# Attention operands as two float32r stacks on half the partitions each, scores and maxima in alternating row tiles, three score banks, and outputs kept transposed

## What is computed

```python
x = x + _layernorm(_L0_attn_ref(_layernorm(x), qkv_w, qkv_b, out_w, out_b))
x = x + _layernorm(_L0_ffn_ref(_layernorm(x), W1, b1, W2, b2))
...
# _L0_attn_ref: 16 heads of 16
qkv = x @ qkv_w.T + qkv_b
scores = einsum('bhqd,bhkd->bhqk', q, k) / sqrt(16)
attn = softmax(scores, axis=-1)
out = einsum('bhqk,bhkd->bhqd', attn, v)
return out.reshape(B, S, E) @ out_w.T + out_b
```

## Time and profile before

| | us |
|---|---|
| median of 3 runs | 2549.8 (2549.22 to 2554.26) |
| the profiled execution | 2556.4 |
| its span, first to last instruction | 2554.6 |
| phase_qkv | 0 to 119 |
| phase_attention, first instruction at 119.5, first scores at 175.3 | 119 to 987 |
| phase_project_ffn | 987 to 1250 |
| the rest | 1250 to 2555 |

### The profile page before, as it was taken

One profiled execution on the slowest core, in us unless ns is written; L12 is line 12 of the kernel. 1 busy time (PEld: TensorE's weight loads), 2 busy tenths in 40 slices (PEclk: granted clock), 3 DMA queues, 4 the chain that ended last, 5 costly groups with the idle time before them and its releaser, 6 DMA issues. The chain is left out here.

```text
span 2554.6 us, 41316 instructions
## 1 busy us (share of the span) xinstructions
PE 2278.0 (89%) x14644; PEld 1462.9 (57%) x14644; DVE 1613.1 (63%) x2762; ACT 1345.3 (53%) x2589; POOL 644.6 (25%) x407
## 2 busy tenths in 40 slices
PE   7779999999999994787579999999999999588886
PEld 4412222222222222676568888888888888477775
DVE  5588788877878852677435445454545534568876
ACT  5517777777777773454254344444434444354551
POOL 3400000000000000355423325233332523234432
PEclk9859999999999997898789999999999999799998
DMA  6831211211121002111330213121220311200100
GB/s 193 241 77 54 55 40 39 73 41 39 39 73 41 6 7 88 34 50 50 120 100 26 93 38 105 52 67 52 67 93 28 115 51 59 66 17 26 33 17 25
DMA packets 129296, 159.02 MB, mean 62 GB/s; under 512 B 29896, under 2 KB 111952, under 8 KB 125008
## 3 DMA queue, kind: packets, MB, share of 16 engines
q1 hardware_dynamic: 129104, 156.47, 20.6%
HBM read 117.76 MB, written 38.27 MB: 61 GB/s over the span
## 5 line engine op out<-in xcount | busy, mean ns | idle before, releaser
L509 DVE TENSOR_REDUCE att_sb_mx<-att_ps_psM 128x1 f32<-128x1024 f32 x512 | 608.4, 1220 | 151.0 <-PE att_ps_psM L567 143.7
L667 ACT ACTIVATE att_sb_pt<-att_ps_psS 128x512 f32<-128x512 f32 x1024 | 586.2, 598 | 209.4 <-PE att_ps_psS L574 193.7
L574 PE MATMUL att_ps_psS<-att_sb_q,att_sb_k 99*128 99x512 bf16 x1024 | 392.7, 386 | 30.5 <-ACT att_sb_pt L667 12.0
L574 PEld LDWEIGHTS att_ps_psS<-att_sb_q,att_sb_k 99*128 99x128 bf16 x1024 | 96.9, 96 | 458.4 <-ACT att_sb_pt L667 406.4
L567 PE MATMUL att_ps_psM<-att_sb_k,att_sb_q 96*128 96x512 bf16 x1024 | 321.2, 396 | 28.5 <-DVE att_sb_ident_b L503 23.2
L582 PE MATMUL att_ps_psO<-att_sb_pt,att_sb_v 128*32 128x512 f32 x2048 | 273.9, 607 | 1.0 <-ACT att_sb_pt L667 1.0
L163 POOL MEMSET ffn_sb_half<- 128x4 f32 x1 | 0.1, 107 | 853.5 <-POOLq L184 853.5
L1922 ACT ACTIVATE gla_sb_sg<-gla_ps_psP 128x512 f32<-128x512 f32 x64 | 38.2, 598 | 277.1 <-PE gla_ps_psP L1683 277.1
L2256 POOL TENSOR_TENSOR gla_sb_dm<-gla_sb_dm,gla_sb_masked 128x1024 f32<-128x1024 f32 x64 | 158.5, 2498 | 90.5 <-DMA gla_sb_dm<-decay_rows 90.2
L1939 ACT ACTIVATE gla_sb_dm<-gla_sb_dm,gla_sb_neg_g 128x128 f32<-128x128 f32 x512 | 156.4, 391 | 10.1 <-POOL gla_sb_dm L2256 10.1
L567 PEld LDWEIGHTS att_ps_psM<-att_sb_k,att_sb_q 96*128 96x128 bf16 x1024 | 99.1, 100 | 107.7 <-DVE att_sb_mx L509 31.3
(11 more groups left out here) (256 smaller groups left out, 4917.0 us busy)
## 6 DMA issues: line engine op xcount, KB each, us to landing
gla_sb_dm<-decay_rows SPq DMA_DIRECT2D x32, 1024.0 KB, 5.8
gla_sb_eg<-decay_exp SPq DMA_DIRECT2D x64, 256.0 KB, 6.7
qk_parts<-qkv_sb_part SPq DMA_DIRECT2D x64, 192.0 KB, 3.1
values<-qkv_sb_va SPq DMA_DIRECT2D x32, 256.0 KB, 3.5
att_sb_v<-values SPq DMA_DIRECT2D x32, 256.0 KB, 3.7
att_sb_q<-qk_parts SPq DMA_DIRECT2D x32, 192.0 KB, 3.1
att_sb_k<-qk_parts SPq DMA_DIRECT2D x32, 192.0 KB, 3.0
qkv_sb_xin<-in_x SPq DMA_DIRECT2D x8, 512.0 KB, 5.1
```

The costliest lines, as they stand in the source:

```text
L509: nc.vector.tensor_reduce(mx[:, t // NT, t % NT:t % NT + 1], psM[:, t % 2, :], AX.X, ALU.max).then_inc(maxima_free, 1)
L574: pe.matmul(psS[:, j % 2, :], k[0:ROWS, g, j, s * P:(s + 1) * P], q[0:ROWS, g, qh, j, :], start=True, stop=True).then_inc(scores_done, 1)
L667: nc.scalar.activation(pt[:, s % 2, j, :], psS[:, j % 2, :], ACT.Exp).then_inc(exp_done, 1)
```

## The change

- phase_qkv multiplies in float32r: weights and turned inputs are split in a high and a low part, and three passes (high x high, high x low, low x high) replace one float32 matmul. q and k leave in two float32r parts in place of three bfloat16 ones, the low one made by DVE from PSUM; GpSimd's part falls away. `part` has two buffers. The scale of 1/4 moves to the exponential.
- phase_attention stacks three blocks of 16 rows (48) and two rows of maxima, 50 in all, once on partitions 0 to 49 and once on 64 to 113: heads 0 and 2 of a group below, 1 and 3 above. The k side has -1 on the rows of the maxima, set by memsets ahead of the loads.
- Each step issues scores in the order of heads 0, 2, 1, 3, and behind each of them one half (512 keys) of a maxima tile on the other row half. L582's group stands behind the third of them. psS has three banks; the maxima's rows are turned into one of these at step 5.
- Maxima run one and a half units ahead.
- GpSimd splits the maxima in two parts. Outputs are not turned: SP spreads the row of sums over partitions (four DMAs), DVE takes the reciprocal, SP stores it in DRAM and reads it back spread over 32 partitions for each head (four DMAs), and GpSimd multiplies `osb` with it. SP stores the result as it lies, features on partitions.
- phase_project_ffn reads its operand turned already; `turn_projected` and `copy_projected` go.

```diff
-Q_PART = (0, 1, 2, 0, 0, 1)
-K_PART = (0, 1, 0, 1, 2, 0)
+Q_PART = (0, 0, 1)
+K_PART = (0, 1, 0)
-ROWS = STACK + 3
+ROWS = STACK + 2
+HALF_PE = P // 2
...
+        PASSES = ((whi, xhi), (whi, xlo), (wlo, xhi))
...
                     for k in range(KD):
-                        mm = pe.matmul(psQ[:, mt, :], w[:, k, mt * P:(mt + 1) * P], xT[:, u, k, :],
-                                       start=(k == 0), stop=(k == KD - 1))
+                        for p, (wp, xp) in enumerate(PASSES):
+                            mm = pe.matmul(psQ[:, mt, :], wp[:, k, mt * P:(mt + 1) * P], xp[:, u, k, :],
+                                           start=(k == 0 and p == 0), stop=(k == KD - 1 and p == 2))
...
-        part = m.sb("part", [P, 4, 3, ST], BF16)
+        part = m.sb("part", [P, 2, 4, 2, ST], F32R)
...
-        q = m.sb("q", [P, NG, QH, HG, ST], BF16)
-        k = m.sb("k", [P, NG, HG, SEQ], BF16)
+        q = m.sb("q", [P, NG, QH, 2, ST], F32R)
+        k = m.sb("k", [P, NG, 2, SEQ], F32R)
-        psS = m.ps("psS", [P, 2, ST])
+        psS = m.ps("psS", [P, 3, ST])
-        psX = m.ps("psX", [P, NT, P])
...
+            def sums(u, w):
+                sp.wait_ge(osb_ready, u + 1)
+                for j in range(HG):
+                    sp.dma_start(den[VW * j:VW * (j + 1), w, :], osb[VW * j:VW * j + 1, w, :]).then_inc(den_in, 16)
+                sp.wait_ge(rden_ready, u + 1)
+                sp.dma_start(dens[w].rearrange("(p c) -> p c", p=P), rden[:, w, :]).then_inc(rden_out, 16)
+                sp.wait_ge(rden_out, 16 * (u + 1))
+                for j in range(HG):
+                    sp.dma_start(rb[VW * j:VW * (j + 1), w, :],
+                                 dens[w, j * ST:(j + 1) * ST].rearrange("(a c) -> a c", a=1).to_broadcast([VW, ST])
+                                 ).then_inc(rb_in, 16)
...
+            def body(b, g, last):
+                for qh in range(QH):
+                    start = isinstance(b, int) and b == 0 and g == 0 and qh == 0
+                    pb, pg, pq = (b, g, 0) if qh else ((b, g - 1, 1) if g else (b - 1, NG - 1, 1))
+                    if not start:
+                        sums(unit(pb, pg, pq), pq)
+                    nb, ng = (b, NG - 1) if g == 0 else (b + 1, g - 1)
+                    if qh == 0 and not (isinstance(nb, int) and nb >= BATCH):
+                        load_first(nb, ng, minus_set[ng] if start else None)
+                        load_second(nb, ng)
+                    if not (last and qh == 1):
+                        rows(*unit_after(b, g, qh), None if start else unit(pb, pg, pq))
...
+                    if not start:
+                        out(pb, pg, pq)
...
+            def maxima_half(b, g, qh, t, c):
+                u = unit(b, g, qh)
+                r, j, n = 1 - t % 2, t // 2 // NT, t // 2 % NT
+                rs = slice(HALF_PE * r, HALF_PE * r + STACK)
+                if c == 0:
+                    wait_past(pe, maxima_taken, TILES * u + t - 1)
+                mm = pe.matmul(psM[:, t % 2, c * ST:(c + 1) * ST], q[rs, g, qh, j, n * P:(n + 1) * P],
+                               k[rs, g, j, c * ST:(c + 1) * ST], start=True, stop=True)
+                if c == QH - 1:
+                    mm.then_inc(maxima_done, 1)
...
+            def scores(b, g, qh, s, i, turning):
+                u, pos = unit(b, g, qh), place(s, i, turning)
+                r, j = ORDER[i] % 2, ORDER[i] // 2
+                rs = slice(HALF_PE * r, HALF_PE * r + ROWS)
...
+                pe.matmul(psS[:, ring_slot(pos), :], k[rs, g, j, s * P:(s + 1) * P], q[rs, g, qh, j, :],
+                          start=True, stop=True).then_inc(ring_done, 1)
...
+                        for i in range(HG):
+                            scores(b, g, qh, s, i, not final)
+                            t = AHEAD + 2 * s + i // 2
+                            if t < TILES:
+                                if not final:
+                                    maxima_half(*nxt, t, i % 2)
+                            elif not last:
+                                maxima_half(*nxt2, t - TILES, i % 2)
+                            if i == 2:
                                 if s:
-                                    values(g, u, s - 1)
+                                    values(b, g, qh, s - 1)
...
+            def normalize(u, w):
+                pool.wait_ge(rb_in, 64 * (u + 1))
...
+                nc.gpsimd.tensor_tensor(on[:, w, :], osb[:, w, :], rb[:, w, :], ALU.mult).then_inc(on_ready, 1)
```

More of the change, by code:

```diff
@@ L265, in _ @@
             s = Steps(LN)
[L266 to L272, removed]
@@ L284, in body @@
+            stats_of_x(0, 0)
+            normalize_x(0, 0)
+            dve.wait_ge(whi_ready, 1)
+            nc.vector.tensor_tensor(wlo[:, :, :], w[:, :, :], whi[:, :, :], ALU.subtract).then_inc(wlo_ready, 1)
+            take_turned(0, 0)
+            dve.wait_ge(b_ready, 32)
+            dve.wait_ge(va_set, 4)
             def body(i, u, last):
                 if not last:
[L286 to L300, removed]
+                    stats_of_x(i + 1, 1 - u)
@@ L302, in _ @@
+                for mt in range(2):
+                    low_part(i, u, mt)
+                if not last:
+                    normalize_x(i + 1, 1 - u)
+                for mt in range(2, 4):
+                    low_part(i, u, mt)
+                if not last:
+                    take_turned(i + 1, 1 - u)
+                for pair in range(2):
+                    take_values(i, u, pair)
             over_supertiles(dve, body)
@@ L539, in _, with reciprocal @@
-            for qh in range(QH):
-                maxima(0, 0, qh, range(TILES))
-                split_maxima(0, 0, qh)
+                    if t == 0 and not (isinstance(u, int) and u < 2):
+                        dve.wait_ge(split, 2 * (u - 1))
+                    nc.vector.tensor_reduce(mx[:, qh, 8 * r + c:8 * r + c + 1], psM[:, t % 2, :], AX.X,
+                                            ALU.max).then_inc(maxima_taken, 1)
+            def reciprocal(u, w):
+                dve.wait_ge(den_in, 64 * (u + 1))
+                nc.vector.reciprocal(rden[:, w, :], den[:, w, :]).then_inc(rden_ready, 1)
@@ L660, in body, with exponentials @@
+            def exponentials(u, s, i, turning):
+                pos = place(s, i, turning)
+                act.wait_ge(ring_done, HG * (KT * u + s) + i + 1)
+                if i == 0:
+                    wait_past(act, pv_done, KT * u + s - 1)
+                nc.scalar.activation(pt[:, s % 2, ORDER[i], :], psS[:, (pos + 1) % 3, :], ACT.Exp,
+                                     scale=AD ** -0.5).then_inc(ring_taken, 1)
+            copy_rows(0, 0)
             def body(b, g, last):
                 for qh in range(QH):
-                    u = 2 * (NG * b + g) + qh
+                    u = unit(b, g, qh)
+                    start = isinstance(b, int) and b == 0 and g == 0 and qh == 0
+                    final = last and qh == 1
@@ L670, in body @@
-                        if s == 3 and not (last and qh == 1):
-                            copy_rows(u + 1)
+                        if s == TURN_AT and not final:
+                            copy_rows(u + 1, (HG * s + 1) % 3)
+                        for i in range(HG):
+                            exponentials(u, s, i, not final)
+                            if s == 0 and i == 2 and not start:
+                                copy_outputs(u - 1, 1 - qh)
             over_pairs(act, body)
-            copy_outputs(2 * NBG - 1)
+            copy_outputs(2 * NBG - 1, 1)
@@ L998, in _ @@
         def _(act):
-            def copy_projected(i):
-                for k in range(KD):
-                    act.wait_ge(a_turned, KD * i + k + 1)
-                    if k == 0 and not first(i, 1):
-                        act.wait_ge(a_done, i)
-                    nc.scalar.copy(aT[:, k, :], psT[:, k, :]).then_inc(aT_ready, 1)
             def take_turned(i, u):
```

482 lines of the change are left out of this document (236 added, 246 removed).

## The result

The changed kernel takes 2655.1 us (median of 4 executions, 2638.6 to 2657.2; a fifth took 2663.3), the kernel before 2551.1 beside it: a ratio of 1.040, 95% interval 1.036 to 1.045. The forecast was 2577, with 2525 to 2630 around it. The direction was right, the size was not: +104 us where the sum had +27. The profiled execution after is the fastest of its four (2638.6, span 2636.9), so its stages explain 82 of the 104. It is set against the 2554.6 of the earlier trace rows.

What follows compares the result with a forecast made beforehand. The old attention step was taken as bound by a chain through ACT and PE over two score banks, not one engine. Terms +4 - 17 + 29 + 9 + 10 - 8 = +27 us on 2549.8 gave 2577 us, range 2525 to 2630.

Steps and rivals of the forecast that it cites:

- The attention step: Attention loop, one key tile of four heads and 512 queries: 3.25 us after the change against 3.05, +29 us in all.
- the ring: Attention loop, closed once per step: second half of an odd maxima tile, reduction, next odd first half, L582, second half; 3.25 us.
- Rival C: Attention step: f32r scores and maxima serialise without pairing, ring 3.59 us, 244 x 0.34 = 83 more, 2651 us; chance 0.11.
- Rows of the maxima: SP's queue in units with loads: rows issued behind loads land late, about 0.8 us for 12 units, +9 us.
- The 0.9 us of slack: Attention loop: time the next unit's first scores can wait for their rows before the ring needs them.
- Attention start: From the attention stage's first instruction to its first scores: fewer reductions and no held DVE cast, -17 us (-11 to -19).
- Normalisation: End of attention: sums, reciprocal, store, broadcasts and GpSimd's multiply exposed, 15 us where 4.8 was, +10 us (+6 to +14).
- FFN: Feed-forward stage: first turn and copy go, later transposes and copies counted at 0.9, -8 us (-3 to -13).
- QKV: QKV stage: PE's gain from three f32r passes hidden behind larger DMA transfers, +4 us (-3 to +9).
- B: Attention step, faster rival: weight loads are fetched ahead, ring 3.04 us, 2533 us in all; chance 0.22.
- D: Attention step, faster rival: banks never bind, step falls to ACT's chain of 2.6 us, 2438 us in all; chance 0.09.
- the odd bank: Attention loop: the one of psM's two banks holding odd maxima tiles, to which the bound moves from the score banks.

## Why the forecast was right or wrong, point by point

- *The attention step*, 3.25: right (3.27), each link too. With the loads out of the way the loop is 849.5 us, where the sum had 835. Of the 14 over it, 5 are the step (244 x 0.02), 3 are the turn of the loop over the batch (a unit of 29.2 where 26.1 is normal), and 5 are the last unit at half clock (25.6 where 20.5 is normal). The values' place shows that it was the ring, the version without pairs that pairing is part of it. Rival C's price for it, 0.34 a step, was too high: 0.20.
- *Rows of the maxima*, +9: this is the step that failed. Its mechanism was right (order of sums, loads, rows in SP's queue, and a wait in 12 units) and its size wrong, by the versions with and without it: 50.7 us in the profiled executions (900.2 less 849.5), 64.5 in the medians. Two things were mis-sized.
  - The wait: 3.0 us a unit (36.0 over 12) and not 0.8. The 18 loads took 12.3 us; the reckoning had 10, although its own row, six loads in 4.08 us, makes 12.2 of eighteen. Counted from the first scores of the unit above, at 438.74, the loads end at 25.0 (said: 24), the rows are issued until 27.9 (26.5), and the scores that need them start at 29.2 (28), where they could have started at 26.2. And even as it stands the reckoning gives 28 less 26 less 0.9, 1.1 us and not 0.8. The 0.9 us of slack doesn't show: the three shortest waits, 2.0 to 2.6 us, made their units 2.6 to 2.8 longer.
  - The clock, which the sum put at nothing: it took each microsecond of wait as one microsecond of time, also at the far end of its bounds (2.5 us a unit, +30). PE's 12 waits add up to 36.0 us and the loss to 50.7 in the same execution, and waits filled with work gave 26 us back. The trace of before has the case too. At its turn of the loop over the batch the step at 575.3 reads 6.15 us and the next one 4.46, in place of 3.05:

```profile
580.07 0.39 PE L574 MATMUL att_ps_psS<-att_sb_q,att_sb_k 99*128 99x512 bf16 x1 [2.73 <-issue]
```

- *Attention start*, -17: right (-14.8).
- *Normalisation*, +10: right (+8.5). The chain from the copy at 1057.59 to the output's issue is the one worked out; it takes 13.3 us to the next stage, where the forecast had 15:

```profile
1058.20 2.41 SPq L492 DMA_DIRECT2D att_sb_den<-att_sb_osb  x4
1061.75 0.25 DVE L548 RECIPROCAL att_sb_rden<-att_sb_den 128x16 f32<-128x16 f32 x1 [20.17 <-DMA att_sb_den<-att_sb_osb]
1062.04 0.34 SPq L494 DMA_DIRECT2D sums<-att_sb_rden  x1
1063.46 1.72 SPq L497 DMA_DIRECT2D att_sb_rb<-sums  x4
1067.05 1.26 POOL L727 TENSOR_TENSOR att_sb_on<-att_sb_osb,att_sb_rb 128x512 f32<-128x512 f32 x1 [19.43 <-DMA att_sb_rb<-sums]
1068.34 0.36 SPq L502 DMA_DIRECT2D attended<-att_sb_on  x1
```

- *FFN*, -8: wrong, +0.9. The turn that went was work in a wait. The first projection started 10.3 us into the stage before (997.12 less 986.8) and starts 9.6 into it now, as it waits for the weights and the bias:

```profile
1081.05 1.22 PE L978 MATMUL ffn_ps_psA<-ffn_sb_wo,ffn_sb_aT 128*128 128x256 f32 x2 [23.53 <-DMA ffn_sb_b_o<-in_out_b]
```

  The bias is issued 2.4 us into the stage now and 1.5 before, behind one more load of the attended tile. The later transposes and copies, of which I had counted nine tenths as time, were beside other work: from projection to projection the last three steps over the supertiles take 27.2 to 27.3 us before, and 27.3 to 27.4 after.
- *QKV*, +4: -2.6, within the bounds. The queue is still nearly full, but it moves more in the same time, as the forecast had thought possible with larger packets: from 60 to 84 us (packets, MB, share)

```profile
q1 hardware_dynamic: 7419, 7.04, 94.2%
```

  in place of 8938 packets and 6.46 MB, 293 GB/s where it was 269. No run took it apart further. Its miss of 7 us and the miss of 9 in the feed-forward stage go against each other in the total; that is luck.
- *Rivals.* B and D did not come: the ring is 3.26 and not 3.04 (pairs are 0.33 and 0.24 apart), and the odd bank binds. D's step of 2.6 came when the values left the ring. So the rule of the Trainium skill behind D (TensorEngine Tiling (Array Packing), "Theoretical Speedup") did not come out in the time: the pairs overlap, as it says, and a step gains 0.20 us of 3.47, not a factor near two.
- *The range* ended at 2630 because no case in it joined the expected step with rows later than 2.5 us a unit and the clock behind them.

## What to carry to other kernels

A DMA queue whose engine also carries the small copies that PE waits for is a schedule: write down its idle places in a unit and put the bulk loads into them, and ask of every moved load which of the waits behind it now comes last (here first the rows, then the sums, and with them DVE's whole queue). Price a wait of PE at more than its length, for the clock behind it: here 50.7 us for 36.0 of waiting, and some 50 for 12.4 in the version with the rows first. And take the time of a queue from a row, load by load: the earlier trace rows had 0.68 us for each load, and 18 of them are 12.2. Where two halves of a tile share a bank, keep long work from between them: the same instructions with the values one place later gave 0.66 us of 3.27 a step.

## What the runs showed of the hardware that was not expected

- Matmuls that compute nothing can pay: 12 in each wait gave back 26 us and raised the granted clock from 0.88 to 0.94 in the same stretch.
- Short waits are enough for the clock to fall. In the changed kernel all twelve waits on the rows (2.0 to 4.1 us) are followed by a stretch at 0.50, and in the version with the rows first all seven of 1.1 to 2.2 us. How long it stays there differs widely: 17.1 us behind one of 2.2, 6.8 behind the turn's gap with pairs and 71.7 without, with PE busy for 68.15 of these. And it can fall without such a gap: the version with loads in the gaps and the values behind dropped to 0.50 in its last units in one profile of two, with no gap of PE over 0.5 us from 800 us on. What decides it these runs don't tell.
- Pairs on the two halves of the partitions gain 0.20 to 0.24 us in a step of four (float32r, 48 and 50 rows, 512 columns). In the ring the reduction (1.28 us) and the values (1.00) stay as they are.
